# Experts' row transposes stand between up and down products, their copies in halves, and the first gate product has 320 columns

## The reference

```python
E, I, K, CAP = 64, 256, 8, 256
scores = sigmoid(tokens @ router_w)
# the best 4 of 8 groups of experts, in them the best 8 experts per token, weights topk_w
dispatch[flat_e, pos_c] += tokens[tidx] * valid      # up to 256 rows of each expert, in order of token
g = einsum("ech,ehi->eci", dispatch, gate_w)
u = einsum("ech,ehi->eci", dispatch, up_w)
expert_out = einsum("eci,eih->ech", silu(g) * u, down_w)
output[tidx] += expert_out[flat_e, pos_c] * topk_w * valid
```

## Time and profile before

| | |
|---|---|
| median of the runs | 1304.29 us (lowest 1303.26, highest 1367.09, 3 runs) |
| the profiled execution | 1306.46 us |
| span of its instructions | 1304.7 us, 22618 instructions |
| mean granted clock of PE | 0.995 |

### The profile page before, as it was taken

The page is one execution under the profiler, slowest core; times in us unless marked ns, Lnnn a source line. Parts: engine busy times, 40 slices in busy tenths (PEclk is TensorE's granted clock), DMA queues, the critical chain, the costliest instruction groups (busy, mean ns, idle before and its releaser), DMA issues.

```text
span 1304.7 us, 22618 instructions
## 1 busy us (share of the span) xinstructions
PE 1282.5 (98%) x7591; PEld 1128.0 (86%) x7591; DVE 913.6 (70%) x1786; ACT 650.7 (50%) x1061; POOL 432.7 (33%) x344
## 2 busy tenths in 40 slices
PE   8999999999999999999999999999999999999994
PEld 7888888888888888888889999999999999999994
DVE  7887787867878678785556667666766666676661
ACT  5422233222232222322256787777777777778772
POOL 1000000000000000000014766666767666676753
PEclk9999999999999999999999999999999999999997
DMA  8346554565545655435447999999999999999995
GB/s 290 97 139 154 128 135 109 144 167 127 126 106 142 167 134 124 103 107 135 136 131 242 272 293 288 288 292 286 286 284 290 292 289 292 286 288 293 290 268 65
DMA packets 203800, 263.65 MB, mean 202 GB/s; under 512 B 49268, under 2 KB 138744, under 8 KB 203768
## 3 DMA queue, kind: packets, MB, share of 16 engines
q1 hardware_dynamic: 175096, 191.93, 51.1%
q0 software_dynamic: 28672, 71.32, 23.5%
HBM read 178.18 MB, written 71.39 MB: 191 GB/s over the span
## 4 chain that ended last, share of the span: by engine, by line
PE 98%; DMA 1%; POOL 0%; issue 0%; DVE 0%; ACT 0%; SPq 0%
PE pmm L1265 18%; PE pmm L1263 18%; PE pmm L1264 18%; PE pout L1263 11%; PE pout L1265 11%; PE pout L1264 11%; PE ptr L1498 4%; PE plp L1327 2%; PE plp L1356 1%; PE plp L1336 1%; PE ptr L1275 0%; DMA xbuf<-_L_attn_proj_matrix_dram 0%; DMA out_dram<-outs,slot_cols 0%; POOL out_dram L1624 0%; PE plp L1345 0%
## 5 line engine op out<-in xcount | busy, mean ns | idle before, releaser
L1624 POOL DMA_INDIRECT out_dram<-outs,slot_cols x128 | 226.0, 1766 | 166.4 <-DMA out_dram<-outs,slot_cols 142.7
L1263 PE MATMUL pmm<-xt_hi,proj_hi 128*128 128x256 f32 (+1 forms) x776 | 249.5, 322 | 1.0 <-DVE xt_lo L805 1.0
L1265 PE MATMUL pmm<-xt_hi,proj_lo 128*128 128x256 f32 (+1 forms) x776 | 246.6, 318 | 0.0
L1264 PE MATMUL pmm<-xt_lo,proj_hi 128*128 128x256 f32 (+1 forms) x776 | 246.6, 318 | 0.0
L1263 PE MATMUL pmm<-xt_hi,sgu_hi 128*128 128x256 f32 (+1 forms) x768 | 246.1, 320 | 0.2 <-issue 0.2
L1264 PE MATMUL pmm<-xt_lo,sgu_hi 128*128 128x256 f32 (+1 forms) x768 | 243.4, 317 | 0.0
L1265 PE MATMUL pmm<-xt_hi,sgu_lo 128*128 128x256 f32 (+1 forms) x768 | 243.4, 317 | 0.0
L1608 POOL TENSOR_TENSOR earlier<-earlier,chosen 128x64 bf16<-128x64 bf16 x64 | 24.3, 379 | 614.9 <-DVE chosen L926 611.1
L1614 POOL DMA_INDIRECT xbuf<-rows,slot_cols x128 | 177.3, 1385 | 82.4 <-issue 39.2
L555 ACT ACTIVATE feat<-pmm,ab 128x512 f32<-128x512 f32 x66 | 45.4, 687 | 286.5 <-PE pmm L1265 286.5
L1264 PEld LDWEIGHTS pmm<-xt_lo,proj_hi 128*128 128x128 f32 x776 | 147.8, 190 | 10.2
(11 more groups left out here) (196 smaller groups left out, 2562.6 us busy)
## 6 DMA issues: line engine op xcount, KB each, us to landing
raw<-in_L_ffn_gate_w_dram SPq DMA_DIRECT2D x64, 512.0 KB
raw<-in_L_ffn_up_w_dram SPq DMA_DIRECT2D x64, 512.0 KB
raw<-in_L_ffn_down_w_dram SPq DMA_DIRECT2D x64, 512.0 KB
outs<-in_L_attn_x_dram SPq DMA_DIRECT2D x32, 512.0 KB, 4.0
out_dram<-outs SPq DMA_DIRECT2D x32, 512.0 KB, 3.3
xbuf<-in_L_attn_x_dram SPq DMA_DIRECT2D x52, 256.0 KB, 7.5
raw<-xn SPq DMA_DIRECT2D x52, 256.0 KB, 6.2
rows<-raw SPq DMA_DIRECT2D x39, 256.0 KB, 4.2
```

What stands on the lines that cost most here:

```text
L1263: pe.matmul(psum, lh, rh, start=first and n == 0, stop=False)
L1264: pe.matmul(psum, lh, rl, start=False, stop=False)
L1265: ins = pe.matmul(psum, ll, rh, start=False, stop=final and n == len(pairs) - 1)
L1624: pool.indirect_dma_start(out=out, out_offset=bass.IndirectOffsetOnAxis(ap=slot_cols[:, at:at + 1], axis=0), in_=outs[e.b][:, c, :], in_of ...
```

## The change

PE's stage becomes: gate and up of s, look-up, transposes of s+1, down of s-1. In the prologue expert 1's gate and up follow expert 0's without transposes between them. The transposes raise the semaphore `e_turned` twice, after four and after eight, and ACT's and DVE's conversion of `ptr` is two instructions each. ACT's stage starts with silu, then next weights, next rows, hidden, output, and last the down weights. DVE takes the gate half of the next weights first, then hid, then the rows, then the up half. The first of the 24 gate products covers 320 columns: `xt_hi` from the expert's 256 columns on and 64 behind them, whose results land in the columns of `pmm[0]` that the second block starts anew.

The diff, cut to its core:

```diff
...
 E_COLS = slice(48, 48 + CAP)
+E_LEAD = 64
 WARM = 26
...
             def e_turned_hi(e):
-                act.wait_ge(e_turned, e.n + 1)
-                act.activation(xt_hi[e.b][:, :, E_COLS], ptr_e, copy).then_inc(e_xt_hi_made, 1)
+                for half in range(2):
+                    at = slice(2 * half, 2 * half + 2)
+                    act.wait_ge(e_turned, 2 * e.n + half + 1)
+                    act.activation(xt_hi[e.b][:, at, E_COLS], ptr_e[:, at], copy).then_inc(e_xt_hi_made, 1)
 
...
 
-            def stage(e, next_rows=True, next_weights=True, out_prev=True, look=None):
+            def stage(e, next_rows=True, next_weights=True, out_prev=True, look=None, first=False):
+                e_silu(e)
+                if next_weights:
+                    gate_up_hi(e.next())
                 if next_rows:
                     e_turned_hi(e.next())
-                if next_weights:
-                    gate_up_hi(e.next())
-                e_silu(e)
-                down_hi(e)
                 e_hidden_hi(e)
+                if first:
+                    for b in range(2):
+                        act.wait_ge(out_stored[b], 16 * GROUPS)
                 if out_prev:
                     e_out(e.prev())
+                down_hi(e)
                 if look is not None:
...
             stage(turn(0), next_weights=False, out_prev=False)
-            for b in range(2):
-                act.wait_ge(out_stored[b], 16 * GROUPS)
-            stage(turn(1))
+            stage(turn(1), first=True)
             with act.Fori(0, CHUNKS - 2) as m:
...
             def e_turned_lo(e):
-                dve.wait_ge(e_xt_hi_made, e.n + 1)
+                dve.wait_ge(e_turned, 2 * e.n + 2)
                 slot_weights(e)
-                dve.tensor_tensor(xt_lo[e.b][:, :, E_COLS], ptr_e, xt_hi[e.b][:, :, E_COLS].bitcast(F32),
-                                  ALU.subtract).then_inc(e_xt_lo_made, 1)
+                for half in range(2):
+                    at = slice(2 * half, 2 * half + 2)
+                    dve.wait_ge(e_xt_hi_made, 2 * e.n + half + 1)
+                    dve.tensor_tensor(xt_lo[e.b][:, at, E_COLS], ptr_e[:, at],
+                                      xt_hi[e.b][:, at, E_COLS].bitcast(F32),
+                                      ALU.subtract).then_inc(e_xt_lo_made, 1)
 
...
             def stage(e, next_rows=True, next_weights=True, look=None):
+                if next_weights:
+                    gate_up_lo(e.next(), (0,))
+                e_hidden(e)
                 if next_rows:
...
                 if next_weights:
-                    gate_up_lo(e.next())
-                e_hidden(e)
+                    gate_up_lo(e.next(), (1,))
+                e_hidden_lo(e)
                 down_lo(e)
-                e_hidden_lo(e)
                 if look is not None:
...
             output(turn(GROUPS - 1), 3)
-            stage(turn(0), next_weights=False)
+            e_turned_lo(turn(1))
+            stage(turn(0), next_rows=False, next_weights=False)
             stage(turn(1))
...
         def _(pe):
-            def products(psum, pairs, first=True, final=True):
+            def products(psum, pairs, first=True, final=True, lead=False):
 
                 for n, (lh, ll, rh, rl) in enumerate(pairs):
-                    pe.matmul(psum, lh, rh, start=first and n == 0, stop=False)
+                    if n > 0 or not lead:
+                        pe.matmul(psum, lh, rh, start=first and n == 0, stop=False)
                     pe.matmul(psum, lh, rl, start=False, stop=False)
...
                 pe.wait_ge(gathered[e.b], 16 * CB * (e.i + 1))
-                at_least(pe, e_xt_lo_made, e.n)
+                at_least(pe, e_xt_lo_made, 2 * e.n)
                 for h in range(HB):
...
                                            ident[:])
-                ins.then_inc(e_turned, 1)
+                    if h % 2 == 1:
+                        ins.then_inc(e_turned, 1)
 
             def e_gate_up(e, parts=(0, 1)):
-                pe.wait_ge(e_xt_lo_made, e.n + 1)
+                pe.wait_ge(e_xt_lo_made, 2 * (e.n + 1))
                 at_least(pe, e_hid_made, e.n)
...
                               for h in range(HB)]
+                        lead = m == 0 and i == 0
+                        if lead:
+                            pe.matmul(pmm[m][:, 0:CAP + E_LEAD], egu_hi[e.b][:, at[0]],
+                                      xt_hi[e.b][:, 0, E_COLS.start:E_COLS.stop + E_LEAD], start=True, stop=False)
                         ins = products(pmm[m][:, i * CAP:(i + 1) * CAP], [
                             (egu_hi[e.b][:, at[h]], egu_lo[e.b][:, at[h]], xt_hi[e.b][:, h, E_COLS],
-                             xt_lo[e.b][:, h, E_COLS]) for h in range(HB)])
+                             xt_lo[e.b][:, h, E_COLS]) for h in range(HB)], lead=lead)
                     ins.then_inc((e_gate_done, e_up_done)[m], 1)
...
             e_gate_up(turn(0), (1,))
+            e_gate_up(turn(1))
             pe.wait_ge(out_free, 2 + J * GROUPS)
             e_turn(turn(2))
-            e_gate_up(turn(1))
             e_down(turn(0))
...
                     e = four(2 * m + 1, k)
-                    e_turn(e.next())
                     e_gate_up(e)
...
                         look_up(m + 2)
+                    e_turn(e.next())
                     e_down(e.prev())
             for n in range(E - 6, E - 1):
+                e_gate_up(turn(n))
                 e_turn(turn(n + 1))
-                e_gate_up(turn(n))
                 e_down(turn(n - 1))
...
```

## The result

The changed kernel takes 1313.89 us (median of 4 runs, 1313.18 to 1317.76) against 1304.28 for the kernel before in the same session: 1.0078 of its time, 95% interval 1.0065 to 1.0091. So it is 10 us slower, within 2%. The forecast was 1323.0 with 1304 to 1340.

A forecast was written before the change was run, and what follows sets the result against it. PE, 98% busy, was taken to set the end, with transfers close behind. Profiled 1306.46 + 1.75 (wider product) + 0.9 (first experts) + 16 (stalls) = 1325.1, with the median 2.2 below the profiled run: 1323 us, range 1304 to 1340.

The forecast's parts named there:

- What bounds the kernel: PE sets the end, transfers close behind; a reordering saves only if products follow each other faster.
- Place of the transposes: Transposes moved in front of the down products: 0 to +0.01 us per expert, taken as 0.
- The product of 320 columns: First gate product 64 columns wider: 0.027 us each, 1.75 us over 64 experts, bounds 0 to 7.
- First and last expert: PE idle about 1.1 us before expert 1's gate products, +0.9 once; last down block 3 us later, hidden.
- Ordinary stages and sign sums: Ordinary stages do not stop, 0.85 us spare; behind sign sums PE is 0.2 too late, 14 times: 2.5 us.
- The weight loads: Late down copy delays up loads; room 11.8 to 9.4 us, about 9.3 with count loads; all stalls taken as 16.
- The sum: Whole kernel: 1306.46 + 1.75 + 0.9 + 16 = 1325.1 us profiled, so 1323 for the median.
- loads keep up: Experts' stage: landings shrink by 2 to 3 us, only the sign sums' 2.5 is left: 1309.5 us; chance 0.28.
- The clock: Rival, experts' stage: 14 stops each lead to half a stage at 1.2 GHz, adding 32 us: 1355; chance 0.02.

The follow-up runs named there:

- e4: Changed kernel with only the first eighth of the down weights of experts 2 to 63 loaded: 1302.08 us, ratio 0.9970 to the kernel before.
- e9: Changed kernel with only the first 128 of each expert's 256 output rows scattered: 1300.70 us, ratio 0.9960 to the kernel before.
- e8: Changed kernel with gate and up loads issued before down, ACT's down copy ahead of the outputs, sign sums split over two stages: 1296.42 us, ratio 0.9944.
- e11: Changed kernel with the 16 sign sums of a look-up split into 8 and 8 over two stages, nothing else: 1316.64 us, ratio 1.0106.
- e1: Changed kernel with an ordinary first gate product of 256 columns: 1317.97 us, ratio 1.0085 to the kernel before.
- e6: Changed kernel with SP issuing gate and up of expert n+1 ahead of down of expert n: ratio 1.0007, ten runs between 1300.55 and 1342.77 us.
- e13: The kernel of e8 without the split of the sign sums: 1304.48 us, ratio 0.9976, ten runs in two heaps.
- e2: Kernel before with the first gate product widened to 320 columns and nothing else changed: 1305.50 us, ratio 0.9980.
- e12: The kernel of e8 with a first gate product of 272 columns instead of 320: 1306.23 us, ratio 1.0008 to the kernel before.
- e10: The kernel of e8 with a first gate product of 256 columns, no wider one: 1304.32 us, ratio 0.9995 to the kernel before.

## Why the prediction was right in its verdict, and where its steps were off

*What bounds the kernel.* Right that PE alone set the end, with the transfers close behind. "A reordering can only save on PE if the products themselves follow each other faster" was meant to close the matter, and it was what happened. No row of before has the wider product, but that one pace is not all there is could be seen there. Expert 1's block in the earlier trace rows begins at 694.86, behind 0.18 us of idle, and ends here:

```profile
700.39 0.39 PE L1263 MATMUL pout<-sdn_hi,hid_hi 128*128 128x512 f32 x1
```

That is 5.53 us, and without the first interval of 0.19 it is 0.1135 for each of the other 47, the fast pace; the 61 blocks like that of the earlier trace rows have 5.74.

*Place of the transposes.* 0.31 at the first down product, taken as 0.32. Nothing lost at the gate, nothing at the look-up (0.46 instead of 0.43 us). Correct, apart from the pace.

*The product of 320 columns.* The term of +1.75 had the right size for the product itself, 0.03 each. The failed step is its bounds, "0 and +0.11", with nothing below zero, and with it "I take 0" for a change of neighbours: with a down product ahead of it, the block is 0.25 us shorter than before. Of this 0.05 was in the working (0.08 for the neighbour, less 0.03 for the width), and 0.20 is the pace. This is the term that was mis-sized: +1.75 where the account gives -9.2, net of the blocks that lost the pace and of 1.4 for the clock.

*First and last expert.* 0.9 idle, predicted 1.1; the last down block 3.03 late, predicted 3, and hidden behind the scatters ahead of the last expert's.

*Ordinary stages and sign sums.* No stops in ordinary stages, 0.19 behind sign sums 13 times, predicted 0.2 x 14. Not foreseen: behind such a gap the gate and up block is 0.1 to 0.3 us longer than the fast one; this is part of the -9.2.

*The weight loads.* Right in mechanism and place: down issued late, at phase 12.4 (1018.22 against a stage that began at 1005.86) where 12.6 was said; four of the five stops at the end of the second stage behind a look-up's, as worked out, and one a stage later. e4, e9 and e8 confirm it from three sides. (The room "from 11.8 to 9.4" is 11.6 to 9.4 by its own terms, 2 x 9.27 + 2.2 - 9.1, which changes nothing.) The size was 16, of which 2.5 for sign sums and 13.5 for loads; the five stops cost 8.1 and the fallen clock 1.4. The step that failed took six of the 14 turns with count loads at 11.8 us from issue to landing, against a room of 9.3. In the trace of the changed kernel these 14 up loads took 6.2 to 9.5 us in ten turns and 10.8 to 12.3 in four. PE stopped for just these four, and landing less stop is 9.7 to 9.9 in each: fewer late loads, and half a microsecond more room. The fifth stop belongs to a load of a later stage, issued at 1229.49, that took 13.2 us.

*The sum.* I had +18.65; the experts' stage measured +10.8. By terms: the product 10.9 too high, the stops (16 against 8.1 + 2.5) 5.4 too high; the down blocks 5.0 too low, since I set the 0.09 that each loses behind transposes off against 0.08 at the gate, and the gate's saving is already in the -9.2; the last down block 3.2 too low, of which 1.9 came off again at the end of the kernel. So the forecast stands 9 us above the result, and the rival "loads keep up" (1309.5) stood 4 below: it had the size of the load stops too small, by 8, and the pace missing as well. That the result fell inside the range is in part luck: a pace that the working did not have and stops that it made too long pulled one way, by 16, and the longer down blocks and the stop ahead of the last one pulled the other, by 9.

*The clock.* The chance of 0.02 was for 32 us; one fall of 1.4 us came. The Trainium skill (TensorE: Matmul & The Clock Gate, "HAM oscillation — how this bites in real kernels") describes a kernel in which waits of about 3 to 5 us between bursts cost the clock each round. The stops here are shorter: those of 1.09, 1.10, 1.30 and 1.35 us left it at 1.00 and the one of 2.44 took it down for 3.4 us. Length alone doesn't decide: in e11 the block behind a stop of 2.19 kept its pace and the one behind 2.24 took 7.19; in e1 a stop of 1.79 was followed by a block of 7.28, and one of 2.92 by none such. So these traces agree that waits between products can cost the clock, here already below the waits of that page, and show that not every stop does.

## What to carry to other kernels

When PE is 98% busy, the interval between its products is still a quantity to be measured, and not a constant: compare it in every place where the same block stands behind something else. A reordering that shortens a chain on PE's side can shorten the room that a transfer had; work out for each load the issue, the use and the room between them, first for the stage where most is queued. And a wait that is removed alone may uncover the next one (e6): the three changes of e8 gain 17 us together against the changed kernel, while alone one of them gained 3, one scattered over 40 us and one gained nothing. The late tail counts as well: in e13's profiled run more was lost against e8 behind PE's last product than in front of it.

## What the hardware showed that I had not expected

- Products of 256 columns (128x128 weights, a weight load with each) have two paces, 0.118 and 0.1135 us, and most blocks keep one from end to end; some begin slow and turn fast within ten products. Running on without a gap, the block had the fast one only where its first product is 320 wide and a 512-column product stands directly ahead; not behind transposes (e2), and not with 272 or 256 columns (e12, e10). Behind a delay of 0.03 us or more (e1), and when the clock had come back up (1088.00 to 1090.49 in the changed kernel), narrow blocks were fast too in many cases. What these have in common is a first interval of 0.14 to 0.26 us instead of 0.12; but the blocks behind transposes have 0.20 there and are slow, all but two of the first experts before (690.83, and 694.86 as shown above). Why was not found out.
- A stop of PE of 1.8 to 2.4 us brought the granted clock down in some cases and in others not; in the changed kernel 0.9 us after the restart, in e1 and e11 0.2 us after it, each time for 3.4 us.
- The time in which the same load lands depends on what is issued around it: an up load took 8.4 us from issue to landing in the changed kernel and 6.1 with an eighth of the down loads (e4), by the medians in part 6 of their pages. It is not the transfers' share alone. In e10, where the down load is whole but the weight loads are issued 1.7 to 4 us apart instead of three within 1 to 3 us, it took 6.1 as well, with a share of 1.02 against the 1.01 of the changed kernel, and of 0.92 in e4.
